# The last pair of a two-layer tower split into its two batches on separate streams, and eight heads per bank copy in the second attention

## The chip, the cores and the metric

The kernel runs on one core of one Trainium2 chip. The metric is the device time of one execution in microseconds; lower is better. It is written in Bass: each engine (PE for matmuls, ACT, DVE, POOL, and SP as a DMA queue) gets its own instruction stream in a fixed order, and the engines meet at semaphores. An instruction that waits holds all that is queued behind it on its engine.

## The reference

Eight sequences of 256 tokens by 256 features pass through two layers, each a token mixer and a feed-forward part with a layer norm after each:

```python
h = L0_tok(x)                                  # state-space mixer, 64 states per token
h = layernorm(h + L0_attn(h))                  # causal attention, 8 heads of 32, with a rank-one bias
# L0_ffn: norm, 32 heads of 8 (full attention), residual, then experts by position:
xe = xf.reshape(2, 8, 128, 256)                # tokens in order: 8 experts of 128 tokens, twice
y  = gelu(xe @ w1[e] + b1) @ w2[e] + b2
h = layernorm(h + y)
# L1_attn: gated linear attention, 4 heads of 32 keys and 64 values, a scan over 256 tokens
S = exp(gk_t) * S + k_t v_t ;  o_t = q_t S ;  o = rmsnorm(o) * gw * silu(g)
h = layernorm(h + o @ Wo)
# L1_ffn: softmax gate over 8 experts (256 -> 1024 -> 256, relu), the best two, weighted
h = layernorm(h + sum_k top_probs[k] * expert[topk_idx[k]](h))
```

All is float32.

## The kernel before

The program has three parts. `s4_tokens` computes the state-space mixer. `main_loop` computes everything up to the gate of the last feed-forward part. `expert_mixture` then runs 39 tiles of 128 gathered token rows through the expert that each tile belongs to, with all eight experts' matrices (16 MB) resident, and combines the two results per token.

`main_loop` works on four pairs of batches (pair p holds batches p and p + 4), 512 tokens each, in four blocks of 128. There are two sorts of work. The attention slots (stream x) handle two heads each: scores, their maxima on DVE (line 1715), transposed scores, exp on ACT (1543), and values (1207). X0 is the causal attention of layer 0 (8 slots per pair), X1 the 32-head attention in its feed-forward part (32 slots per pair, 16 per batch). Side stages are everything else: Y3 (projections for X0), Y2 or Y2d (from X0's output to X1's input), Y1a (X1's output projection, the positional experts' two products with GELU between, layer norm, called h2), Y1b (gated linear attention, its projection and norm, called h3, and the gate with its counts and scatters). `Plan.ORDER` puts the side stages on two streams: a has Y3, Y2 and Y1b of pair 2, b has Y1a and Y1b of pairs 0 and 1, Y1a of pair 2, then Y1a and Y1b of pair 3.

The order of the streams among each other is fixed at build time. `Plan.STAGES` lists the slots of each stage with estimated costs on PE, DVE and ACT and the names of the banks they take; `Plan.needs` lists which slot may only be ordered after which; `Plan.schedule` walks through a model of the three engines and picks at each step the slot that could begin first, among near equals the one with the longest tail. Every engine follows this one order (`weave`). The side stages share two accumulator banks (ps6, ps7), handed out in turn as tickets (`take`, 1260), so a bank's next user waits for the eviction of the user before last, on whichever stream that was.

X1's values of four heads (a quad) are gathered in bank ps4, 32 rows for each. Each quad ends in an ACT copy to `acc` (1534), two PE transposes (`outputs_t`, 1229), a DVE reciprocal of the softmax sums and a product (`normalise`, 1749). POOL prepares padded values of eight heads in `vpad` (`pad`, 1053): eight columns of values and one of ones in 32.

Y1a of pair 3 can only begin when all of X1 of pair 3 is normalised, and Y1b of pair 3 follows it. Where this leaves PE without work, `busy_last` (1281) issues filler matmuls (line 1279), 44 in all, each of 512 columns, seen in the trace as two records. The four 1 MB matrices of a pair's two positional experts pass through the two buffers of `wexp` (`load_w`, 916). The expert matrices of the last part are loaded when h2 of pair 3 and the gate of pair 2 are done (`y1b` of SP, 1016), since their room overlaps buffers of the main loop. After the gate of a pair, POOL scatters its rows into slots by expert, 8 indirect DMAs per pair (1068); the main loop ends when all have landed.

## Time and profile before

| | us |
|---|---|
| median of 3 runs | 1294.23 |
| lowest, highest | 1287.56, 1296.31 |
| the profiled execution | 1290.59 |
| its span, first to last instruction | 1288.8 |
| PE busy in the span | 1076.3 (84%) |
| DVE, ACT, POOL busy | 714.7, 481.5, 239.4 |

The rows further down are from the profiled execution. Times in them count from the start of the span. PE is the matmul part of TensorE, PEld its weight loads, which overlap the matmuls. Busy PE time includes the pipeline's depth, and filler matmuls. PEclk is the granted clock as a share of 2.4 GHz. The main loop lies between about 117 and 966 us, the expert tiles between 967 and 1252.

### The profile page before, as it was taken

The numbers are of one execution on the slowest core, as the hardware profiler recorded it, in microseconds if no ns is written. First come the engines' busy times: TensorE is split into PE (matmuls) and PEld (weight loads), VectorE is DVE, ScalarE is ACT, GpSimd is POOL, SyncE is SP. The second block draws the span as 40 slices with busy tenths as digits, with TensorE's granted clock in tenths as the row PEclk, the third lists the DMA queues.
The fourth block names the chain that finished last, engine by engine and source line by source line (L and its number), as shares of the span: only waits on it lengthen the run. The fifth ranks groups of instructions, "written<-read, shape, count | busy, mean of one in ns | idle before, by whom it ended". The sixth has DMA issues, their size and how long they took to land. (4 is left out here: it accounts for less than half of the span.)

```text
span 1288.8 us, 23098 instructions
## 1 busy us (share of the span) xinstructions
PE 1076.3 (84%) x8482; PEld 771.6 (60%) x8482; DVE 714.7 (55%) x1793; ACT 481.5 (37%) x970; POOL 239.4 (19%) x269
## 2 busy tenths in 40 slices
PE   1227997987999888889988988888889999999990
PEld 1124665544666456666455654674548999999980
DVE  7992444565555766747677556355443444444445
ACT  2111332444465443346533565343003333333332
POOL 3960000000000001201011100012123333333320
PEclk7557998988999989889987999798889999999995
DMA  5023141018521479122805220022941111111105
GB/s 170 18 52 127 65 183 33 17 37 161 67 75 63 184 218 112 35 67 74 164 1 83 64 93 1 1 66 84 379 159 34 34 42 34 41 36 38 38 30 200
DMA packets 73421, 108.90 MB, mean 84 GB/s; under 512 B 16592, under 2 KB 58336, under 8 KB 72864
## 3 DMA queue, kind: packets, MB, share of 16 engines
q1 hardware_dynamic: 66192, 74.75, 23.2%
q0 software_dynamic: 5280, 14.57, 3.5%
q10 hardware_dynamic: 1840, 18.10, 3.4%
q8 instruction: 71, 1.16, 0.4%
q14 instruction: 38, 0.31, 0.1%
HBM read 83.47 MB, written 40.97 MB: 97 GB/s over the span
## 5 line engine op out<-in xcount | busy, mean ns | idle before, releaser
L1715 DVE TENSOR_REDUCE mx<-scores_ps 128x4 f32<-128x1024 f32 (+1 forms) x160 | 186.8, 1168 | 89.3 <-PE scores_ps L1190 45.0
L1543 ACT ACTIVATE pt<-turned_ps 128x1024 f32<-128x1024 f32 (+1 forms) x160 | 157.9, 987 | 152.7 <-PE turned_ps L1186 92.2
L2255 PEld LDWEIGHTS x_ps<-x_xtT,x_w1s 128*128 128x128 f32 x1248 | 145.3, 192 | 3.4 <-ACT x_xtT L2283 1.5
L2255 PE MATMUL x_ps<-x_xtT,x_w1s 128*128 128x128 f32 x1248 | 145.9, 275 | 1.0 <-ACT x_xtT L2283 1.0
L2269 PE MATMUL x_ps<-x_experts,x_hT 128*128 x624 | 141.0, 379 | 0.0
L2269 PEld LDWEIGHTS x_ps<-x_experts,x_hT 128*128 128x128 f32 x624 | 115.6, 190 | 14.1
L1176 PE MATMUL turned_ps<-q,k 32*128 32x256 f32 x512 | 69.2, 346 | 31.1 <-DVE mx L1715 14.9
L1176 PEld LDWEIGHTS turned_ps<-q,k 32*128 32x128 f32 x512 | 42.1, 196 | 85.1 <-issue 47.2
L2298 ACT ACTIVATE x_hT<-x_ps,x_b1c 128x128 f32<-128x128 f32 x312 | 84.9, 382 | 16.9 <-issue 13.8
L2318 DVE COPY x_w1s<-x_experts 128x2048 f32 x39 | 55.5, 1424 | 49.5 <-PE x_ps L2255 37.4
L2343 DVE TENSOR_TENSOR x_y<-x_ps,x_b2b 128x256 f32<-128x256 f32 x39 | 16.5, 424 | 113.2 <-PE x_ps L2269 113.2
L1225 PE MATMUL ps<-pt,vpad 128*32 128x256 f32 x1024 | 78.5, 430 | 0.6 <-issue 0.6
L2283 ACT COPY x_xtT<-x_ps 128x256 f32<-128x256 f32 x39 | 14.5, 372 | 166.3 <-PE x_ps L2234 166.3
L1060 POOL COPY vpad<-v 128x64 f32<-128x64 f32 x64 | 13.1, 235 | 328.7 <-PE ps L1225 313.7
L2222 POOL DMA_INDIRECT y_rows<-x_y,x_row x39 | 39.2, 1006 | 180.3 <-DVEq L2348 180.3
L1164 PE MATMUL scores_ps<-k,q 32*128 32x256 f32 x512 | 69.3, 348 | 2.0 <-DVE mx L1715 1.2
L481 PE MATMUL s_ps<-s_pw,s_cs 64*32 64x64 f32 x512 | 14.7, 298 | 63.1 <-DVEq L383 58.7
L1397 PE MATMUL ps<-wexp,hid 128*128 128x256 f32 x256 | 61.7, 395 | 3.2 <-issue 3.2
L2212 POOL DMA_INDIRECT x_xt<-x_slots,x_source x39 | 59.8, 1532 | 16.9 <-issue 11.6
L1385 PE MATMUL ps<-tt_b,wexp 128*128 128x256 f32 x256 | 61.2, 389 | 0.4 <-DVE tt_b L1785 0.4
L1397 PEld LDWEIGHTS ps<-wexp,hid 128*128 128x128 f32 x256 | 49.6, 198 | 13.9 <-issue 6.8
L1186 PE MATMUL turned_ps<-mrow,pick 32*128 32x512 f32 x256 | 55.6, 419 | 0.0
(423 smaller groups left out, 1971.2 us busy)
## 6 DMA issues: line engine op xcount, KB each, us to landing
x_slots<-x_slots ACTq DMA_DIRECT2D x4, 4160.0 KB
wexp<-in_L_ffn_w SPq DMA_DIRECT2D x16, 1024.0 KB, 5.6
x_experts<-in_L_ffn_W SPq DMA_DIRECT2D x16, 1024.0 KB, 13.7
q<-heads SPq DMA_DIRECT2D x48, 128.0 KB, 5.3
k<-heads SPq DMA_DIRECT2D x48, 128.0 KB, 9.8
ha<-h SPq DMA_DIRECT2D x16, 256.0 KB, 3.2
x_pair<-y_rows SPq DMA_DIRECT2D x4, 1024.0 KB, 8.9
heads<-nat_k_hi SPq DMA_DIRECT2D x12, 256.0 KB, 4.1
```

Of the source, the lines that this page charges most:

```text
L1164: last = mm(bank[:, qb * T:(qb + 1) * T], q1[r, u.bb, u.tile, qb * P:(qb + 1) * P], k1[r, u.bb, u.tile, :], start=True, stop=True)
L1176: mm(bank[:, kt * T:(kt + 1) * T], k1[r, v.bb, v.tile, kt * P:(kt + 1) * P], q1[r, v.bb, v.tile, :], start=kt == 0, stop=False, skip_group ...
L1186: mm(bank[:, :].rearrange("p (k n) -> p k n", k=2), which, rows.unsqueeze(1).to_broadcast([32, 2, T]), start=False, stop=True, skip_group_ ...
L1225: last = mm(rows[:, 0:T], vpad[:, (pads[w.group] - 1) % 2, kt, w.n, :], data[:, kt * T:(kt + 1) * T], start=kt == 0, stop=kt == 1)
L1385: last = mm(bank[:, (f % 2) * T:(f % 2 + 1) * T], w1[:, c, f * P:(f + 1) * P], mv_[c], start=c == 0, stop=c == DC - 1)
L1397: last = mm(bank[:, 0:D], hid[:, e, f, bb * P:(bb + 1) * P], w2[:, f, :], start=f == 0, stop=f == FT0 - 1)
L1543: sc.activation(pt[v.index // 2 % (PT_RING // 2)][:, :, 0:wide], turned_ps[:, :, 0:wide], ACT.Exp)\
L1715: v.tensor_reduce(mx[:, u.group % 2, 0:blocks, u.n:u.n + 2].rearrange("p b n -> p n b"), scores_ps[:, :, 0:blocks * (P if u.causal else T) ...
L2212: g.indirect_dma_start(out=xt[:, i % XR, :], out_offset=None, in_=xs[:, :], in_offset=bass.IndirectOffsetOnAxis(mx.source[:, i:i + 1], 0))\
L2255: last = mm(ps[2 * (i % 2) + f // KH][:, f % KH * P:(f % KH + 1) * P], w1s[:, i % 2, c, f * P:(f + 1) * P], xtT[:, i % 2, c, :], start=c = ...
L2269: last = mm(ps[4 + (i - 1) % 2][:, 0:D], hT[:, (i - 1) % 2, f, :], w2[:, bass.ds(last_expert, 1), f, :], start=f == 0, stop=f == FT - 1)
L2298: sc.activation(hT[:, i % 2, f, :], ps[2 * (i % 2) + f // KH][:, f % KH * P:(f % KH + 1) * P], ACT.Relu, bias=b1c[:, bass.ds(expert * FT + ...
```

## The change

It has two parts.

In X1, two quads (eight heads) share one bank. POOL writes the values of heads 4 to 7 of a group into columns 16 to 23 of their 32, with the ones in column 24, and zeros stand elsewhere; PE adds the second quad's products onto the first's (`begins`), and only the end of the group leads to a copy, transposes, one reciprocal over 16 sums, and two products.

Pair 3 is divided into its two batches, parts 3 and 4, with stages Z1a and Z1b that work on two blocks of 128 tokens in place of four. Batch 0 stays on stream b; batch 1 goes to a new stream c. They use halves of the same buffers (`hid_half`, `lin_half`, halves of tt_b, yb_b, ob), with semaphores of their own per stream. The second expert's matrices of pair 3 go into `qk0` and `v0`, whose users are done by then, so both batches find all four resident. The expert matrices of the last part are loaded when both h2 and the gate of pair 2 are done. 36 fillers remain, on part 4 alone.

```diff
-             "b": (("Y1a", 0), ("Y1b", 0), ("Y1a", 1), ("Y1b", 1), ("Y1a", 2), ("Y1a", 3), ("Y1b", 3))}
+             "b": (("Y1a", 0), ("Y1b", 0), ("Y1a", 1), ("Y1b", 1), ("Y1a", 2), ("Z1a", 3), ("Z1b", 3)),
+             "c": (("Z1a", 4), ("Z1b", 4))}
...
-        after("Y1b", 2, 18, "Y1b", 3, 3)
-        after("Y1b", 2, 22, "Y1b", 3, 21)
-        after("Y1b", 2, 26, "Y1b", 3, 23)
+        for bb in range(2):
+            after("X1", PAIRS - 1, 16 * bb + 15 + AV_LAG + 2, "Z1a", PAIRS - 1 + bb, 0)
+            after("Y1b", 2, 18, "Z1b", PAIRS - 1 + bb, 3)
+        after("Y1b", 2, 26, "Z1b", 3, 19)
+        after("Y1a", 2, 21, "Z1a", 4, 0)
+        after("Z1b", 3, 22, "Z1b", 4, 19)
...
     def w_slot(p, i):
+        if p == PAIRS - 1 and i >= 2:
+            return (qk0_[:, :, :, :].rearrange("p a c n -> p (a c n)") if i == 2 else
+                    v0_[:, :, :, :].rearrange("p b h n -> p (b h n)")), sg(f"w_last{i % 2}"), 16
...
-            if 4 * p + i >= 2:
+            if p == PAIRS - 1 and i >= 2:
+                sp.wait_ge(sg("av_done"), plan.base["X0", PAIRS - 1] + 16)
+            elif 4 * p + i >= 2:
...
+                if (stage, q) == ("Z1b", PAIRS):
+                    sp.wait_ge(sg("h2_b"), PAIRS)
+                    sp.wait_ge(sg("h2_c"), 1)
+                    sp.wait_ge(sg("slots"), PAIRS - 1)
+                    mixture.load_experts(sp)
...
             for kt in range(2):
-                last = g.tensor_copy(vpad[:, n % 2, kt, :, 0:8],
-                                     v1[:, unit.third, kt, unit.head * 8:unit.head * 8 + 64]
-                                     .rearrange("p (h d) -> p h d", d=8))
+                for e in range(2):
+                    at = (unit.head + 4 * e) * 8
+                    last = g.tensor_copy(vpad[:, n % 2, kt, 4 * e:4 * e + 4, 16 * e:16 * e + 8],
+                                         v1[:, unit.third, kt, at:at + 32].rearrange("p (h d) -> p h d", d=8))
...
-            if k:
+            begins = u.causal or not u.ends_group
+            if k and begins:
                 pe.wait_ge(sg("acc"), k)
...
                         last = mm(rows[:, 0:T], vpad[:, (pads[w.group] - 1) % 2, kt, w.n, :],
-                                  data[:, kt * T:(kt + 1) * T], start=kt == 0, stop=kt == 1)
+                                  data[:, kt * T:(kt + 1) * T], start=begins and kt == 0,
+                                  stop=u.ends_group and kt == 1, skip_group_check=True)
...
                 u = plan.last(s, AV_LAG + 2)
-                if u and u.ends_quad:
+                if u and u.ends_out:
                     outputs_t(u)
...
-        def busy_last(p, n):
-            if p == PAIRS - 1:
-                busy(ps[0], n)
+        def busy_last(part, n):
+            if part.last:
+                busy(ps[5], n)
...
-            busy_last(p, 8)
-            pe.wait_ge(sg("g_o"), p + 1)
-            yield from project(p, "p2", ob, wt.gwo, side)
+            busy_last(part, 5)
+            pe.wait_ge(sg("g_o_" + side), turn)
+            yield from project(q, "p2", ob, wt.gwo, side, blocks)
```

In Z1a each bank takes four hidden slices of 128 tokens in place of two of 256, so a batch's expert half still fills two banks of 512 columns where the pair filled four.

## Rows read from the trace of the kernel before

**Rows 1.** By stretch: busy us of PE, PEld, DVE, ACT, POOL; PEclk; DMA

```profile
207.00:767.00 560.00, 496.58 (x3955) 316.11 (x3953) 346.18 (x802) 265.89 (x412) 44.67 (x89) 0.93 0.38 87
767.00:796.00 29.00, 27.48 (x202) 12.35 (x202) 18.70 (x35) 18.46 (x33) 0.83 (x4) 1.00 0.01 1
796.00:817.50 21.50, 15.87 (x120) 8.22 (x116) 5.84 (x19) 6.79 (x10) 0.00 (x0) 0.60 0.00 0
817.50:866.00 48.50, 45.50 (x224) 38.82 (x224) 24.28 (x51) 21.22 (x31) 3.92 (x2) 0.97 0.14 44
866.00:880.50 14.50, 11.34 (x34) 7.17 (x35) 4.50 (x19) 0.58 (x1) 1.01 (x1) 0.65 0.01 1
880.50:948.30 67.80, 57.44 (x211) 32.79 (x210) 34.31 (x108) 13.44 (x29) 13.86 (x12) 0.87 0.79 280
966.70:1250.00 283.30, 282.24 (x1932) 263.68 (x1933) 128.26 (x340) 99.62 (x352) 97.09 (x76) 0.99 0.12 37
```

**Rows 2.** PE's groups, 817.5 to 966.7: busy us, mean ns, idle before

```profile
L1279 PE MATMUL scores_ps<-ident 128*128 128x512 f32 x88 | 45.8, 675 | 0.8 <-DVE g L1963 0.8
...
L1385 PE MATMUL ps<-tt_b,wexp 128*128 128x256 f32 x64 | 14.4, 381 | 0.0
...
L1302 PE MATMUL ps<-wo,tt_b 128*128 128x256 f32 x16 | 3.9, 384 | 0.9 <-DVE sd L1972 0.9
```

**Rows 3.** Timeline of PE in the tail: start us, length us, line, names, count

```profile
766.97 1.09 PE L1289 MATMUL ps<-ident,hb 128*128 128x128 f32 x8 [2.14 <-DVEq L1822]
...
817.69 1.97 PE L1289 MATMUL ps<-ident,heads_X 128*128 128x128 f32 x8 [0.56 <-DVE heads_X L1757]
...
873.65 7.02 PE L1279 MATMUL scores_ps<-ident 128*128 128x512 f32 x10
...
947.96 0.30 PE L1496 MATMUL ps<-g_both,mask_g 128*128 128x32 f32 x2
...
948.32 15.70 PE L1279 MATMUL scores_ps<-ident 128*128 128x512 f32 x36
...
966.75 0.24 PE L2238 MATMUL x_ps<-ident,x_b1r 64*128 64x64 f32 x1 [2.73 <-PEq L2086]
```

**Rows 4.** Timeline of PE around one pair of output transposes

```profile
744.94 0.44 PE L1236 MATMUL ps<-ident,acc 128*128 128x128 f32 x2
745.31 1.07 PE L1225 MATMUL ps<-pt,vpad 128*32 128x256 f32 x16
```

**Rows 5.** Waits of the weight loads, 207 to 767: us in total, times, longest

```profile
PEld turned_ps L1176 <- DVE mx L1715: 34.6, 32, 2.3
...
PEld ps L1236 <- issue: 17.2, 58, 0.8
```

**Rows 6.** Line 1715 from 740 us on: the last maxima of the last pair

```profile
L1715 DVE TENSOR_REDUCE mx<-scores_ps x14: 1207/1225/1226, 742.4 to 795.7; 128x4 f32<-128x1024 f32 x14
```

**Rows 7.** Chain that ended last: 32 records of 128 columns in the expert stage

```profile
984.26 3.57 PE x_ps L2255 x32
```

**Rows 8.** Timeline of POOL: the two roots of the last linear part

```profile
919.03 2.93 POOL L1097 TENSOR_TENSOR rs_b<-rs_b,mhalf 128x16 f32<-128x16 f32 x1 [15.36 <-DVE rs_b L1984]
...
934.22 1.01 POOL L1097 TENSOR_TENSOR rs_b<-rs_b,mhalf 128x4 f32<-128x4 f32 x1 [12.26 <-DVE rs_b L1806]
```

**Rows 9.** Line 1618, GELU: ns least/median/most, first and last start

```profile
L1618 ACT ACTIVATE hid<-hid,b1c x64: 491/493/511, 360.0 to 857.6; 128x256 f32<-128x256 f32 x64
```

**Rows 10.** DVE's groups by form: a copy and a sum from banks

```profile
L1902 DVE COPY hid<-ps 128x512 f32<-128x512 f32 x32 | 22.1, 691 | 32.1 <-PE ps L1385 30.8 <-POOL rs_a L1097 1.2
...
L1907 DVE TENSOR_TENSOR yb_b<-ps,hb 128x256 f32<-128x256 f32 x16 | 6.8, 423 | 38.0 <-PE ps L1397 37.8 <-DVE ob L1989 0.2
```

**Rows 11.** Line 1071, the last scatters: ns least/median/most, first and last start

```profile
L1071 POOL DMA_INDIRECT x_slots<-hb,g_slot x8: 956/960/1057, 952.2 to 961.2; - x8
```

**Rows 12.** SP's queue: first and last issue of expert matrices

```profile
893.46 0.43 SPq L2132 DMA_DIRECT2D x_experts<-in_L_ffn_W  x1
...
934.41 0.47 SPq L2134 DMA_DIRECT2D x_experts<-in_L_ffn_W  x1
```

More of the change, by code:

```diff
@@ L864, in main_loop, with linear, forward_side, forward_turn @@
     mhalf = sb("mhalf", [P, 16])
-    def linear(p):
-        if plan.side("Y1b", p) == "a":
+    parts = Part.all()
+    def linear(pt_):
+        if pt_.half:
+            return (plan.side("Z1b", pt_.q), *lin_half[pt_.bb])
+        if plan.side("Y1b", pt_.q) == "a":
             return "a", g4_a, qs_a, ks_a, vg_a
         return "b", g4_b, qs_b, ks_b, vg_b
+    def forward_side(pt_):
+        return plan.side("Z1a" if pt_.half else "Y1a", pt_.q)
+    def forward_turn(pt_):
+        return 1 if pt_.last else pt_.q + 1
+    def linear_turn(pt_):
+        side = linear(pt_)[0]
+        return [o.q for o in parts if linear(o)[0] == side].index(pt_.q)
     scores_ps = ctx.enter_context(nc.psum_tensor("scores_ps", [P, 2, 512], fp32))
@@ L1391, in y1a @@
                 pe.wait_ge(sem, count)
-                for bb in range(2):
-                    bank = take(f"down{e}{bb}", p)
+                for i, bb in enumerate(part.bbs):
+                    bank = take(f"down{e}" + ("" if part.half else str(bb)), q)
                     for f in range(FT0):
-                        if bb == 0 and f % 2 == 0:
-                            pe.wait_ge(sg("hidden"), (E_IT * p + e) * FT0 + f + 2)
-                        last = mm(bank[:, 0:D], hid[:, e, f, bb * P:(bb + 1) * P], w2[:, f, :], start=f == 0,
+                        if i == 0 and f % 2 == 0:
+                            pe.wait_ge(sg("hidden_" + side), (E_IT * (forward_turn(part) - 1) + e) * FT0 + f + 2)
+                        last = mm(bank[:, 0:D], h_[:, e, f, i * P:(i + 1) * P], w2[:, f, :], start=f == 0,
                                   stop=f == FT0 - 1)
@@ L1437, in y1b @@
             for h2 in range(NHG // 2):
-                busy_last(p, h2)
-                banks = [take(f"at{2 * h2}", p), take(f"at{2 * h2 + 1}", p)]
-                for tb in range(NTB):
+                busy_last(part, h2)
+                banks = [take(f"at{2 * h2}", q), take(f"at{2 * h2 + 1}", q)]
+                for tb in range(part.n):
                     for i in range(2):
@@ L1669, in y1b @@
+            sc.copy(kT[:, part.bb:part.bb + len(part.bbs), :], full("kt", q)[:, 0:len(part.bbs) * P]
+                    .rearrange("p (b k) -> p b k", k=P)).then_inc(sg("y_act_" + side), 1)
             yield from pause(4)
[L1670 to L1672 removed]
+            for i, bb in enumerate(part.bbs):
+                bank = full(f"o{i}", q)
+                square = tt[side][:, :, cols] if part.half else tt[side][:, bb, :].rearrange("p (b d) -> p b d", b=2)
+                sc.activation(square, bank[:, :].rearrange("p (b d) -> p b d", b=2), ACT.Square).then_inc(sg("y_act_" + side), 1)
@@ L1911, in y1a, with y1b @@
                     yield
-            moments("b", lead("Y1a", p, 20))
+            moments(side, lead(stage, q, len(plan.STAGES[stage]) - 2), blocks, part.at)
             yield
-            normalised("b", h, rs["b"][1])
-            signal("h2")
+            normalised(side, h, rs[side][1][:, part.at:], blocks)
+            signal("h2_" + side)
             yield
-        def y1b(p):
-            side, g4, qs, ks, vg = linear(p)
+        def y1b(part):
+            q, p, cols, blocks = part.q, part.p, part.cols, part.blocks
+            stage = "Z1b" if part.half else "Y1b"
+            roots_at = [k for (z, k) in sorted(plan.ROOTS) if z == stage]
+            side, g4, qs, ks, vg = linear(part)
+            turn = linear_turn(part) + 1
@@ L1989, in y1b @@
-            s.step(v.tensor_tensor(ob[:, :, :], ob[:, :, :], yb[side][:, :, :], ALU.mult))
-            signal("g_o")
+            for n in range(part.n // 2):
+                add_projection("p2", q, n, h, True, side, part.first)
+                yield
+            moments(side, lead(stage, q, roots_at[1]), blocks, part.at)
             yield
-            turned("p2", p, side)
+            normalised(side, h, rs[side][1][:, part.at:], blocks)
+            signal("h3_" + side)
             yield
-            for n in range(2):
-                add_projection("p2", p, n, h, True, side)
-                yield
@@ L1997, in y1b, with gate @@
-            moments(side, lead("Y1b", p, 21))
-            yield
-            normalised(side, h, rs[side][1])
-            signal("h3")
-            yield
-            yield from gate(p, side)
-        def gate(p, side):
-            E = gt.E
-            shape = [P, NTB, E]
-            lo, pr, eq, pre = (z[:, :, :] for z in (gt.lo, gt.pr, gt.eq, gt.pre))
-            m1, m2, ix, dd = (z[:, :] for z in (gt.m1, gt.m2, gt.ix, gt.dd))
+            yield from gate(part, side, stage)
+        def gate(part, side, stage):
+            E, q, p, n = gt.E, part.q, part.p, part.n
+            shape = [P, n, E]
+            lo, pr, eq, pre, oh1, oh2, both = (z[:, 0:n, :] for z in (gt.lo, gt.pr, gt.eq, gt.pre, gt.oh1, gt.oh2, gt.both))
+            m1, m2, ix, dd = (z[:, 0:n] for z in (gt.m1, gt.m2, gt.ix, gt.dd))
```

658 lines of the change are left out of this document (372 added, 286 removed).

## The prediction

> **What bounds the kernel now.** I read the busy table by stage first, then the order of PE's instructions in the late stages, then DVE, ACT and POOL at the places where PE waits.
>
> The table [rows 1] splits the run into four regimes. From 207 to 767 us PE is busy 496.6 of 560 us (89%): attention slots and side stages share it, and PE is near its limit. From 966.7 to 1250 us the expert tiles keep PE busy 282.2 of 283.3 us; the change doesn't touch them. Between lie 200 us in which the pair 3 is finished. From 767 to 796 PE is full (27.5 of 29). From 796 to 817.5 the attention drains: 15.9 of 21.5 us at a clock of 0.60, about 9.5 us of work at full clock. After that Y1a of pair 3 runs beside the end of Y1b of pair 2, with PE full until 866. Then Y1b of pair 3 runs nearly alone: in the 67.8 us from 880.5 PE shows 57.4 busy, but much of that is filler, the matmuls of line 1279. In the whole tail the filler holds PE for 45.8 us [rows 2]. Of this 7.0 us stand at 873.65 and 15.7 at 948.32 [rows 3], so 45.8 - 7.0 - 15.7 = 23.1 us fall into the last chain and its real PE work is 57.4 - 23.1 = 34.3 us, half of the time. So from 866 on the length is set by a chain of dependent steps, not by an engine. The chain starts when the last attention output is normalised (PE takes it up at 817.69) and ends with the count matmuls at 947.96 [rows 3]: 130.5 us. Counted in full-clock work, what remains of PE's real work after 817.5 is about 45.5 x 0.97 = 44.1, plus (11.3 - 7.0) x 0.65 = 2.8, plus 34.3 x about 0.9 = 31: 78 us.
>
> **The second attention's copies.** Each of the 64 quads of X1 ends in one ACT copy, two PE transposes, one DVE reciprocal and one DVE product. After the change this happens once per two quads, with two products: 32 copies, 64 transposes and 32 reciprocals go. The value matmuls stay, in number and shape. On PE one pair of transposes takes 745.31 - 744.94 = 0.37 us between its neighbours [rows 4]; with the wait of its weight loads, 17.2 us in 58 cases or 0.30 us each [rows 5], 0.67. Eight of the 64 quads fall after 767, so 28 removals lie before it: 10.4 us, at most 18.8. But a shorter slot is only worth something where PE holds it; PE also waits for the DVE maxima, 34.6 us in 32 cases [rows 5], and there the gap eats the saving. The bounds are 0 and 18.8; I take **7 us** (two thirds of 10.4). The DVE and ACT savings lie beside PE. POOL's padding copies double in number, but each group of eight heads has its own buffer one group ahead, and POOL is busy 44.7 of 560 us [rows 1]: nothing.
>
> **The first batch is moved under the attention.** Y1a of pair 3 becomes Z1a 3 (batch 0) and Z1a 4 (batch 1). Z1a 3 may start when attention slot 23 of 32 is issued. The last 14 slots have their maxima from 742.4 to 795.7 [rows 6], so slot 23 falls near 763 and Y1a 2 is through by 767: Z1a 3 starts about there. PE work of the whole Y1a 3: 14.4 us up, the same for as many columns down, 3.9 projection [rows 2], and 16 transposes at half of the 0.37 above, 3.0: 36 us; half is 18. The halves lose nothing on PE: 32 records of 128 columns take 3.57 us in the expert stage [rows 7], against 14.4 / 2 = 7.2 us for 32 of 256 columns [rows 2]. The stretch 767 to 817.5 holds 27.5 + 9.5 = 37 us of full-clock work; with 18 more, and four transpose pairs less (1.5), it is 53.5, against 50.5 us now. If PE is full, the attention ends 3 us later; bounds are -3 (the drain sped up by the full clock) and +18 (all of it in front). I take **+3**. The end of attention comes at 817.5 - 7 + 3 = 813.5.
>
> **The second batch's forward part, Z1a 4.** Its PE work is 18 us. Around it stand three evictions of some 1.1 us (a copy of 0.4 to 0.7 [rows 10] and the hand-overs, an estimate), two waits for copy and GELU of 2 us (such a copy and two or three activations [rows 9]), and moments, POOL root (1.01 us for 4 columns [rows 8]) and normalisation, 4 us: 29 us alone. Y1b 2's rest and Z1b 3 run beside it and PE will be full as it is now, so I take **36 us** (bounds 29 and 48.5, which the whole Y1a takes). GELU is cut from 256 to 128 columns, twice the instructions: a 256-column one takes 0.49 us [rows 9]; between 0.25 (no fixed part) and 0.49 (all fixed) I take 0.40, 32 x 0.40 = 12.8 us against 16 x 0.49 = 7.9 us, 5 us more on ACT, which is 21.2 of 48.5 us busy and hides it. Here a rule speaks against the change: the Trainium skill, VectorE: DVE Perf Modes, section The TRN2 errata, says that VectorE and ScalarE pay a fixed extra time per instruction on SBUF sources and wants tiles of 512 elements or more. Its ScalarE row, 224 cycles plus the elements at 1.2 GHz, would make the 128-column GELU an estimated 0.29 us, so ACT would grow by 1.5 us, not 5; no row here shows that shape. On DVE the fixed part is seen: 512 columns take 0.691 us, 256 take 0.423 [rows 10]. Two halves cost 0.16 us more than a whole, but each chain pays only one.
>
> The four matrices of the last pair lie ready, since the second two go into qk0 and v0. Today the last ones are issued as their buffer comes free, and PE doesn't wait for them: it is busy 45.5 of the 48.5 us in which they are used [rows 1]. So residency is worth nothing in itself; it allows two passes.
>
> **The second batch's linear part, Z1b 4.** Now this chain takes 67.8 us. Halving its widths saves half of PE's 34.3 us: 17; of DVE's 34.3 busy us about 13 are gate operations of pair 2 and 3 that keep their size, the other 21.5 fall to 0.6 (0.423 / 0.691): 8.7; ACT, partly beside: 2; the two POOL roots, 2.93 us for 16 columns and 1.01 for 4 [rows 8], are 0.16 us per column, so 1.28 + 0.32 = 1.6. Together 29: **39 us**. Z1b 3 runs beside it. It brings a second gate of about 37 small DVE operations (some 8.5 us, as now), four scatters and what PE work is left, 31 / 2 = 15.5 us less what fits beside Z1a 4. Bank order, DVE and POOL are in-order, so each foreign step in front of the chain delays it. Bounds: 5 us and 39 us (run one behind the other); I take **14**. The seven microseconds of filler at 873.65 disappear within this, since that wait is then filled with work; 44 fillers become 36.
>
> Count matmuls: 813.5 + 36 + 39 + 14 = 902.5 instead of 948.3, **-45.8**.
>
> **From the counts to the experts.** Now eight scatters are issued from 952.2 to 961.2, 1.28 us apart [rows 11], and the first expert instruction of PE comes at 966.75, 4.6 us after the last. Four fewer save 5.1 us. But 18 fillers stay and end at 948.32 + 15.70 = 964.0: they become the bound, 15.7 us after the counts plus 0.3. I take **-2.4**. The 16 MB of expert matrices start with Y1b 2's gate and Z1a 4's end; they are issued 893.46 to 934.41 now, 5.85 us per expert [rows 12], while a tile takes 283.3 / 39 = 7.26 us. Even with a start at 892 the first experts are there at 918; no cost.
>
> **Sum.** -45.8 - 2.4 = -48.2 us on the profiled execution of 1290.6: 1242.4. The median of the runs shown is 1294.2, 3.6 higher: 1246.0. I say **1245**.
>
> **Rivals.**
> *Close packing.* X1 saves 12 us, nothing is lost at its end, Z1a 4 takes 34 and the foreign work adds 7: 817.5 - 12 + 34 + 46 = 885.5, -62.8 - 2.4 = -65: 1229. For it: PE's real work from 755 on is 37 - 1.5 + 78 = 113.5 us, which ends at 868 without gaps. Against: three streams in fixed order through two banks. 0.17.
> *One behind the other.* The X1 saving is eaten by DVE waits, and Z1b 4's steps stand in order behind Z1b 3's: 820.5 + 36 + 39 + 39 = 934.5, -13.8 - 2.4 = -16: 1278. For it: output rows (ob), gate tiles and the running counts are shared, so vg waits for Y1b 2 and the gate of batch 1 for that of batch 0; in the present trace Y1b 2 takes 125 us under interleaving, from 767 [rows 3] to 892, when its end releases the expert loads [rows 12]. Against: its early steps need none of these. 0.20. That the overlap comes to nothing at all (within 1%) is its far end: 0.04 more.
> *Slower, by the clock.* Eight fillers go. Where PE waited on a chain the granted clock was 0.60 and 0.65 [rows 1], where it was full 1.00: these are mixtures of 1.2 and 2.4 GHz. If the tail ran wholly at 1.2 GHz, its 113.5 us would be 227, from 760 to 987: +36, 1331. It turns slower than before only if the mean over that stretch falls under 113.5 / 190.7 = 0.60; now, with half the work density, it is 0.87. The Trainium skill, TensorE: Matmul & The Clock Gate, section What's actually happening, says that half rate is the default and that activity releases the full rate; by that rule denser work should raise the clock, as it did in 817.5 to 866 (0.97). 0.03.
>
> **How the numbers follow.** Forecast 0.56, its own range 1232 to 1262; the rivals 0.17, 0.24 and 0.03. 1228 to 1270 leaves out the lower half of close packing's tail and most of the serial case: 0.8 inside. A measurement of this kernel tells about 1% (13 us) from no change. Faster: 0.56 + 0.17 + four fifths of 0.20 = 0.89; same 0.07; slower 0.04.
>
> **What would show it.** Right: reduction of the maxima of the last pair ends about 10 us before 795.7, up matmuls of 128 columns run before it does; count matmuls of batch 1 near 902; PE busy over 85% until the second batch's g_o; expert start 16 us after the counts. Wrong: X1 stages as long as before (DVE waits grown); more than 50 us between the second h2 and the counts with PE idle behind Z1b 3's gate or a POOL root; or a clock under 0.8 in the tail. The expert stage must stay at 7.26 us per tile.

## The result and the profile after

The changed kernel is slower: median 1308.7 us (1303.2 to 1313.8) against 1290.9 us (1284.0 to 1296.3) of the kernel before on the same chip, ratio 1.014 with a 95% interval of 1.010 to 1.019. The forecast was 1245 us, range 1228 to 1270. The profiled execution spans 1304.8 us, before 1288.8.

First the busy table of the kernel after, the columns as in [rows 1], cut at its own milestones: h2 of pair 2 is taken up by PE at 754.2, the last maxima come at 790.7, the last attention output is taken up at 808.8, h2 of batch 1 at 869.4, the last counts at 961.0.

```profile
207.00:754.20 547.20, 489.05 (x3909) 312.07 (x3909) 342.66 (x776) 259.20 (x385) 53.59 (x149) 0.93 0.39 91
754.20:790.70 36.50, 33.85 (x224) 18.43 (x224) 19.09 (x35) 20.30 (x39) 1.56 (x8) 0.91 0.10 36
790.70:808.80 18.10, 14.29 (x117) 7.15 (x115) 4.72 (x17) 8.28 (x11) 0.00 (x0) 0.91 0.00 1
808.80:869.40 60.60, 49.29 (x266) 37.75 (x267) 26.76 (x58) 23.08 (x49) 4.30 (x3) 0.86 0.00 1
869.40:961.00 91.60, 65.00 (x235) 42.13 (x233) 44.68 (x176) 12.89 (x35) 18.75 (x19) 0.74 0.37 134
985.30:1265.00 279.70, 279.16 (x1920) 263.56 (x1921) 126.08 (x338) 98.31 (x348) 91.16 (x72) 0.99 0.12 36
```

Against [rows 1]: the attention stage got 12.8 us shorter, more than I had taken (7), and the attention ends at 808.8 instead of 817.7. The expert stage is as it was but for some 3 us in its first tiles. The rest is lost between: from the end of attention to the last counts it took 130.3 us before, 152.2 now, and I had forecast 89. PE is busy 65.0 of the last 91.6 us at a granted clock of 0.74, where the single chain of before had 57.4 of 67.8 at 0.87.

The timeline of PE in the tail, the columns of [rows 3]:

```profile
754.20 1.09 PE L1362 MATMUL ps<-ident,hb 128*128 128x128 f32 x8 [2.46 <-DVEq L1926]
...
808.79 0.63 PE L1362 MATMUL ps<-ident,heads_X 128*128 128x128 f32 x4 [0.61 <-DVE yb_b L2017]
...
851.83 0.44 PE L1362 MATMUL ps<-ident,hb 128*128 128x128 f32 x2 [1.98 <-DVEq L1926]
...
860.25 1.97 PE L1362 MATMUL ps<-ident,ob 128*128 128x128 f32 x8
...
869.42 0.60 PE L1362 MATMUL ps<-ident,hb 128*128 128x128 f32 x4
...
921.02 0.64 PE L1577 MATMUL ps<-g_both,mask_g 128*128 128x32 f32 x2 [4.78 <-DVE g_both L2163]
...
947.74 0.61 PE L1577 MATMUL ps<-g_both,mask_g 128*128 128x16 f32 x2 [4.77 <-DVE g_both L2163]
...
961.04 0.40 PE L1577 MATMUL ps<-g_both,mask_g 128*128 128x16 f32 x2 [0.56 <-DVE g_both L2163]
961.28 0.37 PE L1578 MATMUL ps<-g_both,onesr 128*128 128x16 f32 x2
961.51 15.70 PE L1352 MATMUL ps<-ident 128*128 128x512 f32 x36
977.67 0.24 PE L2364 MATMUL x_ps<-ident,x_b1r 64*128 64x64 f32 x1 [0.47 <-PEq L2212]
...
984.14 0.69 PE L2360 MATMUL x_ps<-ident,x_xt 128*128 128x128 f32 x2 [3.45 <-DMA x_xt<-x_slots,x_source]
```

The rows are, in order: h2 of pair 2, the last attention output, h2 of batch 0, the output projection of Y1b 2, h2 of batch 1, and the three gates: pair 2 (32 columns), batch 0, batch 1. The gate of pair 2 comes 33 us later than its 888.2 of before; the three gates follow one another, and PE stands 4.8 us at the head of its queue for each of the first two.

**Where it is lost.** I cut the tail of each trace into stretches of about 4 us and multiplied PE's busy time less filler with the granted clock of the stretch. That gives its work in us at full clock; the rest of its busy time is what the low clock cost. "Copies alone" is the unsplit kernel of the first experiment below, whose attention stage is like that of the kernel after. From h2 of pair 2 to the last counts, us:

| | length | work | low clock | filler | PE idle |
|---|---|---|---|---|---|
| before | 181.0 | 113.2 | 14.1 | 30.0 | 23.7 |
| copies alone | 179.6 | 112.4 | 14.9 | 30.6 | 21.8 |
| after | 206.8 | 117.1 | 23.5 | 21.9 | 44.4 |

The work is about what I had reckoned (113.5). Against the copies alone the tail is 27.2 us longer: 22.6 more of waiting, 8.6 more by the low clock, 4.7 more work, 8.7 less filler. And little of the work moved: under the attention (754 to 809) PE does 43.9 us of it instead of 35.5, but behind the end of attention 74.0 remain of 76.6. Of batch 0's forward part only the first expert got under the attention. Each batch has 64 records of up matmuls; behind 808.8 stand 96, batch 1's own and 32 of batch 0's. PE's groups from 808.8 to 961 (count, busy us, mean ns, idle before):

```profile
L1465 PE MATMUL ps<-tt_b,qk 128*128 128x128 f32 x64 | 9.3, 305 | 0.6 <-DVE yb_b L2017 0.6
...
L1465 PE MATMUL ps<-tt_b,wexp 128*128 128x128 f32 x32 | 3.7, 275 | 0.0
```

**How the chains hold each other.** One place read closely. DVE, ACT and PE each follow one order in which the steps of three chains take turns. On PE's timeline batch 1's output matmuls end at 916.25:

```profile
914.71 1.54 PE L1548 MATMUL ps<-vg_half,g_half 128*128 128x64 f32 x8
```

ACT's timeline at that place, the squares of batch 1 and then the exponential of pair 2's gate:

```profile
916.29 0.60 ACT L1765 ACTIVATE tt_b<-ps 128x512 f32<-128x512 f32 x1 [10.71 <-PE ps L1548]
...
917.25 0.24 ACT L1775 ACTIVATE g_pr<-g_lo 128x32 f32<-128x32 f32 x1
```

DVE's timeline. The product at 913.02 is batch 1's (that of batch 0 came at 896.30); it stands behind DVE's wait for batch 0's root. Then come pair 2's gate, batch 0's two products and the first sum of batch 1:

```profile
910.93 0.19 DVE L2141 TENSOR_TENSOR g_lo<-g_lo,g_m 128x32 f32<-128x32 f32 x1
...
913.02 0.69 DVE L2092 TENSOR_TENSOR ob<-ob,gwb 128x512 f32<-128x512 f32 x1 [1.75 <-POOL rs_b L1170]
917.59 0.18 DVE L2147 TENSOR_REDUCE g_m<-g_pr 128x4 f32<-128x32 f32 x1 [3.88 <-ACT g_pr L1775]
...
920.96 0.68 DVE L2106 TENSOR_TENSOR yb_b<-yb_b,rs_b 128x512 f32<-128x512 f32 x1
...
922.55 0.69 DVE L2099 TENSOR_REDUCE rs_b<-tt_b 128x8 f32<-128x512 f32 x1 [0.17 <-DVE ob L2109]
```

Batch 0's product at 920.96 needs a root that POOL delivered at 913.0. It stands behind pair 2's gate. That gate's exponential needs a result that DVE gave at 911.1, but on ACT it stands behind the squares of batch 1, which wait 10.7 us for batch 1's output matmuls on PE, until 916.3. So batch 0 waits 8 us for pair 2, which waits for batch 1. And batch 1, the last chain, pays too: its squares are there at 916.9, the sum over them comes at 922.55, 5.7 us later, behind pair 2's gate and batch 0's products. No step here is long; each chain pays for the latency of the others. What is shown is the order of the engines' queues. How much the two accumulator banks add, which the three streams share, no run tells apart.

### The profile page after: what moved, and what is told of

It is laid out like the page before. It is cut to its first block and busy times, and to the rows that moved or that the text cites. A ratio compares the mean times of both kernels' runs of the same rounds, so it can differ in the third digit from the quotient of the medians.

```text
span 1304.8 us, 23159 instructions
## 1 busy us (share of the span) xinstructions
PE 1075.9 (82%) x8484; PEld 775.6 (59%) x8484; DVE 717.9 (55%) x1819; ACT 478.1 (37%) x971; POOL 248.8 (19%) x340
## 5 line engine op out<-in xcount | busy, mean ns | idle before, releaser
L2381 PEld LDWEIGHTS x_ps<-x_xtT,x_w1s 128*128 128x128 f32 x1248 | 148.0, 195 | 3.6 <-ACT x_xtT L2409 1.6
L2395 PEld LDWEIGHTS x_ps<-x_experts,x_hT 128*128 128x128 f32 x624 | 115.6, 190 | 14.1
L1134 POOL COPY vpad<-v 128x32 f32<-128x32 f32 x128 | 22.8, 222 | 313.7 <-PE ps L1297 298.9
L1170 POOL TENSOR_TENSOR rs_b<-rs_b,mhalf 128x4 f32<-128x4 f32 (+3 forms) x13 | 17.0, 1309 | 199.8 <-DVE rs_b L1908 145.7
L1465 PE MATMUL ps<-tt_b,wexp 128*128 128x256 f32 (+1 forms) x256 | 53.5, 359 | 0.1
L482 PEld LDWEIGHTS s_ps<-s_pw,s_cs 64*32 64x32 f32 x512 | 11.7, 135 | 64.9 <-issue 37.5
## 6 DMA issues: line engine op xcount, KB each, us to landing
x_experts<-in_L_ffn_W SPq DMA_DIRECT2D x16, 1024.0 KB, 14.1
```

Source lines behind the costliest of these rows:

```text
L1465: last = mm(bank[:, i * wide:(i + 1) * wide], w1[:, c, f * P:(f + 1) * P], mv_[c], start=c == 0, stop=c == DC - 1)
L2381: last = mm(ps[2 * (i % 2) + f // KH][:, f % KH * P:(f % KH + 1) * P], w1s[:, i % 2, c, f * P:(f + 1) * P], xtT[:, i % 2, c, :], start=c = ...
L2395: last = mm(ps[4 + (i - 1) % 2][:, 0:D], hT[:, (i - 1) % 2, f, :], w2[:, bass.ds(last_expert, 1), f, :], start=f == 0, stop=f == FT - 1)
```

## The experiments

Milestones in us of each profiled execution; "attention end" is where PE takes up the last attention output, "h2" where it takes up h2 of the last chain, "Y1b 2" are the counts of pair 2, "first up" is the first up matmul of the expert tiles. Ratios are medians to the kernel before on the same chip, with their 95% interval; executions of one kernel spread over 4 to 18 us, and a profiled one can lie as far as 11 us off its median.

| kernel | h2 pair 2 | attention end | h2 | Y1b 2 | last counts | first up | ratio |
|---|---|---|---|---|---|---|---|
| before | 767.0 | 817.7 | 880.5 | 888.2 | 948.0 | 972.2 | 1 |
| after | 754.2 | 808.8 | 869.4 | 921.0 | 961.0 | 985.3 | 1.014 [1.010, 1.019] |
| e1_heads | 754.3 | 804.4 | 867.4 | 875.1 | 933.9 | 958.2 | 0.982 [0.978, 0.987] |
| e2_split | 764.9 | 817.0 | 877.9 | 929.5 | 969.7 | 993.6 | 1.016 [1.011, 1.021] |
| e3_nofill | 753.4 | 808.1 | 866.6 | 918.2 | 956.3 | 982.6 | 1.008 [1.005, 1.012] |
| e4_linear_first | 755.4 | 834.6 | 883.1 | 888.5 | 965.1 | 987.2 | 1.018 [1.011, 1.025] |
| e5_serial | 761.6 | 841.1 | 931.4 | 902.8 | 977.4 | 999.4 | 1.015 [1.011, 1.019] |
| e6_heads_trim | 752.7 | 803.1 | 859.8 | 870.1 | 928.1 | 952.3 | 0.985 [0.982, 0.988] |
| e7_resident | 755.3 | 805.8 | 868.4 | 876.1 | 932.9 | 957.0 | 0.987 [0.984, 0.990] |
| e8_late_load | 756.3 | 805.8 | 869.5 | 877.2 | 937.2 | 965.1 | 0.992 [0.990, 0.995] |
| e9_forward | 755.5 | 809.8 | 859.5 | 918.8 | 950.1 | 981.0 | 1.006 [1.003, 1.009] |
| e10_no_batch0 | 756.6 | 812.2 | 868.4 | 885.4 | 919.0 | 943.8 | (less work) |
| e11_more_fill | 756.2 | 810.8 | 871.3 | 917.2 | 956.5 | 981.6 | 1.021 [1.014, 1.027] |
| e12_forward_y1b2 | 760.4 | 818.1 | 888.5 | 904.4 | 953.6 | 977.9 | 1.007 [1.004, 1.011] |

**The copies alone, and the split alone.** e1 takes the hunks of the second attention into the kernel before (`vpad` with its nine ones, `ends_out`, `begins`, the 16 sums in `rc`); e2 takes all the others.

> The kernel before with the eight heads per bank copy alone; the last pair stays whole. My step 'X1 copies' said 7 us of gain, with bounds 0 and 18.8. In the profile of the changed kernel h2 of pair 2 comes at 754.2 us where it came at 766.97, so theory A (the copies are worth all of that, the loss lies in the split alone): 12 to 13 us faster than before, near 1278. Rival R (part of the 12.8 us comes from other tail priorities of the order, or is given back where the last chain begins): 0 to 6 us faster.

> The changed kernel with a copy per four heads as before, so the split alone. Theory A (the two parts add up): the split alone costs the 16 to 18 us seen plus the 12.8 us of the copies, so about 29 us slower than before, near 1320. Rival R (the freed slots of the second attention are taken by the first batch's work, so that the copies and the split work together): 18 us slower or less.

The copies are worth 20 us (1274.5 against 1294.2; in e7, on another chip, 17), the split costs 20 (1314.5). Neither is what its theories had (12 to 13 or at most 6 us for the copies, 29 or at most 18 for the split), but the loss is the split's. In e1 the 12.7 us that the copies gain ahead of h2 of pair 2 arrive whole at the experts (14 us earlier); in the kernel after, against e2, 8.3 of 10.7 do. Together the two give +1.4% where their sum would be about 0; I have no run that tells why the copies are worth less beside the split.

**The fillers.** e3 keeps only the 18 behind the counts; e11 lets batch 0's waits have them too.

```diff
-            if part.last:
+            if part.last and n == 18:                             # e3
+            if part.last or part.q == PAIRS - 1 and n < 18:       # e11
                 busy(ps[5], n)
```

> The changed kernel without the 18 filler matmuls that stand in front of the last part's waits; the 18 after its counts stay. The output is the same. Theory F (with three streams the fillers stand in front of other streams' work, which now waits 0.87 to 1.5 us for each; 6.0 us of them stand from 948.6 to 954.5 ahead of the last gate's transposes): 5 to 12 us faster than the changed kernel. Rival C (the clock, 0.56 to 0.87 in the stretches after 869 us, falls further without them): 3 to 15 us slower, with the count matmuls later and the clock in 869 to 961 lower.

> The kernel after with the filler matmuls doubled: those that stand ahead of the waits of batch 1's linear part now also stand ahead of the same waits of batch 0's (18 more, of 0.44 us at full clock each). The granted clock over 869 to 961 was 0.74 in the kernel after. Theory C (the low clock in the tail is what costs): the clock over the linear parts rises to 0.85 or more and the last counts come 5 us or more earlier than 961; ratio to before 1.010 or less. Theory H (PE in order, waits of the chains, not its speed): the clock rises but the last counts come within 3 us of 961 or later, up to 8 us later, since each filler stands ahead of foreign steps; ratio 1.014 to 1.021.

The linear parts of e3 in the busy table (columns of [rows 1]):

```profile
866.60:956.30 89.70, 51.23 (x206) 37.48 (x204) 46.73 (x182) 13.94 (x38) 18.77 (x19) 0.64 0.36 128
```

The same stretch of e11:

```profile
871.30:956.50 85.20, 66.19 (x266) 39.41 (x264) 45.29 (x176) 12.91 (x35) 18.73 (x19) 0.92 0.39 140
```

The clock went from 0.74 to 0.64 and to 0.92, and the chain from 91.6 us to 89.7 and 85.2. So e3 lost clock and no time: its median is 5 us under that of the kernel after, the least that theory F had, with intervals that overlap. The profiled e11 gains 6 us in the chain, but its median of 1313.5 shows no gain (theory C needed a ratio of 1.010 or less; 1.021 is in the range of theory H). How much of the 6 us is real stays open; of the 38 us that this chain took beyond the forecast, a clock of 0.92 gives back 6 at the most.

**The order.** Three kernels keep all the work and change only what waits for what.

```diff
+        after("Y1b", 2, 18, "Z1a", 4, 0)                           # e4
-        after("Z1b", 3, 22, "Z1b", 4, 19)
+        after("Z1b", 3, 22, "Z1b", 4, 0)                           # e5
```

> The changed kernel with one more condition of order: batch 1's forward part (Z1a 4) is ordered only after slot 18 of Y1b 2 (its p2 transposes), so that the linear part of pair 2 is finished earlier. Theory O (three gates in series hang on Y1b 2, whose count matmuls came at 921.0 us where they came at 888.2 before; the order starves it): Y1b 2's counts 15 to 30 us earlier, the last counts 8 to 15 us earlier than 961.0. Rival C (what lengthens the tail is PE at half clock and its idle time as such, not who is first): within 3 us of the changed kernel. Rival W (batch 1's chain was the longest): slower by the 5 to 10 us by which it starts later.

> The kernel after with one more constraint on the order: the linear part of batch 1 (Z1b 4) begins only after the last step of batch 0's (Z1b 3). Nothing is left out. It measures the term of my sum that was 39 us: Z1b 4 alone, from its h2_t transposes to its counts. Theory I (the halves are short, 39 to 45 us alone, and what went wrong is only that three streams wait for each other in a fixed order): Z1b 4 takes 39 to 45 us here; batch 0's counts, without foreign steps, come near 930 instead of 947.7, and the last counts near 972; the kernel is about 11 us slower than after (ratio to before near 1.023). Theory L (a chain of steps keeps most of its length when its tiles are halved): Z1b 4 takes 55 to 62 us alone, of 67.8 for the whole pair in the kernel before; the last counts come near 990 and the ratio is near 1.037.

In e4 pair 2's gate is back at 888.5, yet the last counts come 4 us later, as rival W had it: the attention is pushed back (its last output transposes come at 827.9, 806.0 in the kernel after), and its output is taken up 26 us later. In e5 batch 1's linear part runs alone, from 931.4 to 977.4: 46.0 us. This is the term that I had put at 39 and theory L at 55 to 62. And e5, with the two half chains strictly one behind the other, has the ratio of the kernel after (1.0149, 1.0144): running them side by side gained nothing that can be measured. It isn't a clean test of the linear parts alone, though. The order of the earlier stages changed with the one constraint: the attention's end moved from 808.8 to 841.1, and batch 0's counts came at 925.3, 22 us earlier than in the kernel after.

**Batch 0's linear part left out.** e10 drops Z1b 3 from the order; its 256 tokens have no gate, no scatters and no part in the experts, and its output rows are copies of another batch's.

> The kernel after with the linear part, the gate and the scatters of batch 0 of the last pair left out (its forward part stays; its rows of the output are another batch's, and its tokens are missing among the experts). It asks whose steps stand in front of the last chain, which takes 91.6 us from its h2 transposes (869.4) to its counts (961.0) in the kernel after and 46 when held back until batch 0 is through. Theory Z (batch 0's chain): the last chain takes 42 to 50 us and its counts come at 905 to 918. Theory Y (the rest of Y1b 2, whose counts came at 921): the last chain still takes 60 us or more and its counts come at 930 or later. My forecast of the kernel after had this chain at 39 us with 14 more for batch 0.

Its last chain, timeline of PE:

```profile
868.42 0.60 PE L1363 MATMUL ps<-ident,hb 128*128 128x128 f32 x4
...
903.87 0.66 PE L1363 MATMUL ps<-ident,ob 128*128 128x128 f32 x4 [1.11 <-DVEq L1927]
...
919.01 0.29 PE L1578 MATMUL ps<-g_both,mask_g 128*128 128x16 f32 x2
```

50.6 us instead of 91.6, and pair 2's gate back at 885.4. Theory Z holds, with the end 1 us outside its bounds: batch 0's half chain costs the last one 41 us, where I had 14. That is batch 0's own steps together with the delay that they put on pair 2: Y1b 2's projection comes at 846.9 instead of 860.3 without them, and its counts 36 us earlier; e10 doesn't separate the two. But Z1a 4 still takes 56.2 us (812.2 to 868.4) beside Y1b 2 and the rest of Z1a 3.

**Only the forward part split.** e9 has Z1a 3 and Z1a 4, but one linear chain for the whole pair; its comparison is e6, the unsplit kernel with the same fillers.

```diff
-             "b": (("Y1a", 0), ("Y1b", 0), ("Y1a", 1), ("Y1b", 1), ("Y1a", 2), ("Z1a", 3), ("Z1b", 3)),
-             "c": (("Z1a", 4), ("Z1b", 4))}
+             "b": (("Y1a", 0), ("Y1b", 0), ("Y1a", 1), ("Y1b", 1), ("Y1a", 2), ("Z1a", 3), ("Y1b", 3)),
+             "c": (("Z1a", 4),)}
...
-            after("Y1b", 2, 18, "Z1b", PAIRS - 1 + bb, 3)
-        after("Y1b", 2, 26, "Z1b", 3, 19)
+        after("Y1b", 2, 18, "Y1b", 3, 3)
...
+        after("Z1a", 4, len(self.STAGES["Z1a"]) - 1, "Y1b", 3, 0)
+        after("Y1b", 2, 17, "Z1a", 3, 7)                           # e12 only
```

> Only the forward part of the last pair is split (Z1a 3 under the attention, Z1a 4 after it, all four matrices resident, eight-head copies); its linear part stays whole, one chain for both batches as in the kernel before, with the fillers of the trimmed version (none ahead of h2, 8, 4 and 2 ahead of the later waits). Nothing is left out. Theory I (what costs is that the linear part became two chains that wait for each other; the forward split gains what I forecast for it): end of attention near 809, Z1a 4 some 42 us, h2 of both batches ready near 851 to 858, then about 62 us for the whole chain as in the trimmed unsplit version (859.8 to 928.1 there is 68.3), last counts 915 to 922, 6 to 13 us earlier than that version's 928.1, ratio to before near 0.975. Theory P (the third stream itself costs: it pushes Y1b 2 back, and the vg steps of the last chain wait for it): Y1b 2's output projection comes at 855 to 860 instead of 833, the last counts fall at 926 or later, and the ratio is 0.983 or more.

> The kernel of e9 (forward part split, linear part whole) with one more constraint on the order: the second expert of batch 0's forward part (Z1a 3) waits until the normalised output of Y1b 2 is there, so that Y1b 2 is no longer pushed back by batch 0. In e9 Y1b 2's output projection came at 872.5 and its counts at 918.8, against 832 and 870.1 in the trimmed unsplit version, and the last chain took 90.6 us instead of 68.3. Theory Q (Y1b 2's delay is what lengthens the last chain, and it can be had back without giving the early forward part away): Y1b 2's projection comes at 835 to 848, the last chain takes 66 to 75 us, the last counts come at 922 to 935, ratio to before 0.98 to 0.99. Theory S (the three streams share a fixed amount of time: whatever is put first, another is pushed back by as much): Y1b 2 comes early, but Z1a 4 ends at 875 or later, and the last counts stay at 942 or later, ratio 1.000 or more, as happened when Y1b 2 was put ahead of Z1a 4 in the fully split kernel.

This was the surprise. e9 is 26 us slower than e6 (1298.6 against 1272.1, on different chips; both times the kernel before had 1292): the forward split alone costs more than the split linear part adds to it (10 us, to 1308.7). h2 comes at the same time as in e6 (859.5, 859.8), so the work done under the attention bought nothing, but Y1b 2 is pushed back by 49 us, and the last chain, whose vg steps wait for it, takes 90.6 us instead of 68.3. Theory P, larger than I put it. Its expert loads are late too (issued from 924.6), and from the counts to the experts it takes 30.9 us, 6.7 more than in e6. Two waits of PE in e9:

```profile
872.54 1.97 PE L1364 MATMUL ps<-ident,ob 128*128 128x128 f32 x8 [4.46 <-DVEq L1932]
...
918.75 0.63 PE L1583 MATMUL ps<-g_both,mask_g 128*128 128x32 f32 x2 [4.78 <-DVE g_both L2169]
```

e12 was to give Y1b 2 its turn back, and hardly did: its projection comes at 867.0, 5.5 us earlier than in e9, where e6 has it at 832.0, and its counts at 904.4 against 870.1. The last chain is short again (65.1 us), but Z1a 4 ends 29 us later and the counts come at 953.6. Theory Q is out; of theory S the late end of Z1a 4, the late counts and the ratio are as it had them, the early Y1b 2 isn't. In e4 and e9 what is put first is gained and what is put second is lost, and e12 gained little and lost more. Three orders don't prove that no order pays.

**The two things that I put at nothing.** e7 gives the unsplit kernel the two resident matrices; e8 holds the expert loads back (`filled(sp, "o0", p)` ahead of `load_experts`).

> The kernel before with the eight-head copies, unsplit, and with the one other part of the change that can stand alone: the second expert's two matrices of the last pair go to the memory of qk0 and v0 and are loaded there during Y1a of pair 2, beside the end of the attention. I put that at nothing. Theory N (nothing): Y1a 3 keeps its place and length (transposes at about 804, h2_t at 867), ratio 0.982 as with the copies alone, within 0.004. Theory M (the earlier loads, some 2 MB beside the attention, collide with other transfers, or PE did wait for the late ones): the end of attention moves by more than 2 us or Y1a 3 is shorter by more than 2 us, and the ratio differs from 0.982 by more than 0.004.

> The kernel before with the eight-head copies, unsplit, and with the loads of the sixteen experts' matrices held back until batch 0's output matmuls of the last pair are issued, some 20 us later than they could start, so that they still run when the first expert tile begins, as in the kernel after. Nothing is left out. Theory N (a late load costs nothing while it stays ahead of the tiles, as I put it): from the last counts to the first expert up-matmul 24.2 us as now, and the span as with the copies alone, 1275. Theory D (the load stands in front of the first gathers): the first gather takes about 5.8 us instead of some 3, the first up-matmul comes 26 to 28 us after the counts, and the span grows by 2 to 4 us (ratio 0.984 to 0.986).

e7 equals the copies alone within the intervals: residency is worth nothing, as forecast. e8 is 6 us slower than e7 on the same chip (1281.7 against 1275.6), outside what theory D had. In the traces its counts come 4.3 us later than in e7 and the experts 3.8 us later behind them. Of the 4.3 us, 2.3 are the last gate step, from the transposes of h3 to the counts: 8.5 us in e7, but 10.8 in e8, e1 and the kernel before. The rest I can't account for. POOL's timeline between the last scatter and the first gather, in e1:

```profile
947.17 0.96 POOL L1074 DMA_INDIRECT x_slots<-hb,g_slot  x1 [0.30 <-issue]
953.40 1.74 POOL L2223 DMA_INDIRECT x_xt<-x_slots,x_source  x1 [5.27 <-POOLq L2097]
```

In e8, and PE's first instruction of the expert stage there:

```profile
950.41 0.96 POOL L1075 DMA_INDIRECT x_slots<-hb,g_slot  x1 [0.30 <-issue]
959.91 1.74 POOL L2224 DMA_INDIRECT x_xt<-x_slots,x_source  x1 [8.54 <-POOLq L2098]
...
959.25 0.34 PE L2250 MATMUL x_ps<-ident,x_b1r 64*128 64x64 f32 x1 [6.00 <-PEq L2098]
```

In the kernel after:

```profile
968.71 0.96 POOL L1144 DMA_INDIRECT x_slots<-hb,g_slot  x1 [0.30 <-issue]
978.33 1.73 POOL L2338 DMA_INDIRECT x_xt<-x_slots,x_source  x1 [8.66 <-POOLq L2212]
```

In e4, the split kernel whose last load is issued at 934.43, with the same instruction of PE:

```profile
972.83 0.96 POOL L1145 DMA_INDIRECT x_slots<-hb,g_slot  x1 [0.30 <-issue]
982.26 1.73 POOL L2339 DMA_INDIRECT x_xt<-x_slots,x_source  x1 [8.47 <-POOLq L2213]
...
981.61 0.24 PE L2365 MATMUL x_ps<-ident,x_b1r 64*128 64x64 f32 x1 [0.30 <-PEq L2213]
```

At the end of the main loop all engines meet. In e8 PE is through with its fillers 6.0 us before that point opens, so the scatters hold it up, and they land 3.3 us later than in e1 while the expert matrices stream. In the kernel after the wait of POOL looks the same and isn't: PE's fillers end at 977.21 and the expert stage begins at 977.67, and in e4 and e5, where no expert matrix is under way any more, POOL waits 8.5 and 8.4 us all the same. There the four scatters are early and the 18 fillers behind the counts set the end, as I had forecast. What the late load costs in the kernel after stands behind that. It is issued from 927.95 to 970.56, since it waits for pair 2's late gate ([rows 12]: 893.46 to 934.41), and the first gather takes 5.8 us from its issue to PE's transposes, 3.9 in e1, e4 and e5. From the counts to the first up matmul it is 24.3 us, 22.1 in e4 and 22.0 in e5: 2.2 us.

**Faster than both.** e6, the kernel before with the copies and without the fillers that stood ahead of h2, runs at 1272.1 us, ratio 0.985 [0.982, 0.988].

```diff
-            busy_last(p, 5)
             pe.wait_ge(sg("h2"), p + 1)
...
-            busy_last(p, 6)
+            busy_last(p, 4)
             pe.wait_ge(sg("h3"), p + 1)
...
-            busy_last(p, 4)
+            busy_last(p, 2)
             pe.wait_ge(sg("g_both"), p + 1)
```

> The kernel before with the eight-head copies and without the split, and with fewer filler matmuls in the last pair's linear part: the 5 ahead of the wait for h2 go, the 6 ahead of h3 become 4, the 4 ahead of the gate's result become 2. In the version with all fillers h2 stood ready at about 858.6 and PE took it up at 867.4, behind 6.5 us of filler. Theory F (these fillers stand in the chain): h2_t comes about 6 us earlier and the last counts 7 to 9 us earlier than 933.9; ratio to before near 0.977 against 0.982 with all fillers. Theory K (the fillers hold the clock up, and without them the steps that follow run at a lower clock and give it back): the last counts within 3 us of 933.9, a mean clock over 867 to 934 that is lower by 0.05 or more, and a ratio of 0.982 or above.

Its h2 comes 7.6 us and its last counts 5.8 us earlier than in e1; on one chip it beats the untrimmed e7 by 3.5 us. The fillers ahead of a wait that is already over stand in the chain, as theory F had it, but part is given back: the clock over the last chain is 0.83 instead of 0.87 (e1). The ratio of 0.985 is the one of theory K, and e1 itself (0.982) lies within the interval, so the gain is shown against e7 alone; both are well ahead of the two kernels compared.

## Why the prediction was wrong, point by point

- *What bounds the tail.* Right: from the end of attention on it is a chain of dependent steps. I then computed with the chain as if it were work: I took off the halved busy time of PE, DVE and ACT in full.
- *The copies, 7 us.* Mis-sized: 12.8 us in the attention stage, 0.46 us per removed copy and transposes, inside the bounds of 0 and 18.8. I had cut the saving because PE also waits for the maxima; those waits stayed as they were (33.6 us in 32 cases, 34.6 in [rows 5]), so the gap ate nothing. PE's busy time fell by 7.5 us, the other 5.3 were waiting. e1 puts the whole part at 20 us in the median.
- *The attention's end, +3.* Right: 54.6 us from h2 of pair 2 to it, against 50.1 in e1, so +4.5. But the reason I gave, 18 us of work going in, was wrong: 8 went in.
- *Z1a 4, 36 us.* Failed: 60.6, outside the bounds. The step that failed is "PE will be full as it is now": between 808.8 and 869.4 PE works 49.3 of 60.6 us, and the second half of batch 0's forward part lies in that stretch too. The upper bound of 48.5 was misread as well: it is a stretch of [rows 1] up to 866, while the whole Y1a takes 53.5 us from the attention's end (817.7) until its normalised h2 is there (871.2), and 62.8 until PE takes it up (880.5). So half of Y1a in the new kernel takes as long as all of it did. The 7.0 us of filler at 873.65, which I took for a wait that other work would fill, stood behind h2 already: that wait was over.
- *GELU at 0.40 us for 128 columns.* Right: 32 of them take 0.387 us each (below). The estimate from the Trainium skill, VectorE: DVE Perf Modes, section The TRN2 errata, was 0.29; the measurement decides. Nor was it this that cost the time: behind the attention ACT is busy 36.0 of 152.2 us.
- *Z1b 4 alone, 39 us.* A little low: 46.0 in e5, 50.6 beside Y1b 2 in e10. A half chain is 0.68 of a whole (67.8).
- *Batch 0 beside it, 14 us, bounds 5 and 39.* The largest miss and the step that failed most: 41 us against e10 and 46 against e5, over the upper bound that I took as "one behind the other". It fell on the low side because I counted only what batch 0 adds in work, not that its steps, pair 2's and batch 1's wait for each other in every queue. The kernel with the two half chains in series (e5) is as fast as the one with them side by side.
- *Counts to experts, -2.4.* Right for what I had computed: PE's first expert instruction comes 16.6 us behind the counts, forecast 16.4, before 18.8, and the fillers are the bound. But the first up matmul comes 24.3 us behind them, as before (24.2), since the gather behind that instruction is slow. The step that failed is "even with a start at 892, no cost": the start came at 928, and a load still under way costs 2.2 us here (against e4 and e5); in e8, where it also holds up the scatters, 3.8 in the trace and 6 in the medians.
- *The expert stage*, put at no change: 2.9 us. Its first 32 up matmuls take 6.50 us at a granted clock of 0.56, the next 32 take 3.84 at 1.00, after PE stood 3.45 us for the gather; before, the first took 3.84 too.
- *The sum.* Attention end -4.7, Z1a 4 +24.6, last chain +38.6, counts to experts +2.5, first tiles +2.9: 64 us between -48 and +16.
- *The rivals.* "One behind the other" had the right mechanism in the linear parts (39 + 39 us there; 91.6 measured, 2 x 46) and the wrong floor (1278): it left Z1a 4 at 36 us, and its eaten gain of the copies didn't come. "Slower, by the clock" came out slower, but the lower clock is 8.6 of the 27.2 us, and its mean from 754 to 961 is 0.82, not under 0.60. Beside it no rival had a tail longer than the one before; 0.04 for slower was far too little. Of my signs of being wrong two came: 91.6 us between the second h2 and the counts, and a clock of 0.74 there.

GELU in the kernel after, the columns of [rows 9]:

```profile
L1705 ACT ACTIVATE hid_half<-hid_half,b1c x32: 385/387/403, 784.4 to 846.8; 128x128 f32<-128x128 f32 x32
```

A root of 8 columns on POOL's timeline, 1.64 us (I had taken 0.16 us per column, so 2.93 - 1.28 = 1.65) [rows 8]:

```profile
911.35 1.64 POOL L1170 TENSOR_TENSOR rs_b<-rs_b,mhalf 128x8 f32<-128x8 f32 x1 [18.62 <-DVE rs_b L2104]
```

## What to carry to other kernels

Where a stretch is set by latency, halving the tiles doesn't halve it: here half a chain took 0.68 of a whole, and two of them on engines that work in order took more than the whole (109 us from batch 0's h2 at 851.8 to the last counts, before 67.8). Splitting pays only if the first half truly runs under other work; count first how much of it gets there (here 8 of 18 us) and what it pushes back. To estimate interleaved chains, start from the sum of their lengths alone, not the sum of their work: here 2 x 46 us against 91.6 for the last one. Even that is no upper bound, as the 109 us show. Look also at what the last moved stage releases: a load that starts 35 us later can lie on the path. And where an engine waits at a point where all meet, look at what each of the others does until then before you name the cause.

## What I had not expected of the hardware

- Indirect scatters that end while the 16 MB of expert matrices stream (364 to 399 GB/s in e8) landed late: from the last issue's end to the next step's start 8.5 us in e8 and 8.9 in e9, instead of 5.3 in e1, e7 and e12. In these kernels PE's fillers had ended before. The first gather under the same stream took 5.8 us to PE's transposes in the kernel after instead of 3.9 in e4 and e5.
- The granted clock in the linear tail was 0.64, 0.74 and 0.92 with 0, 19 and 31 us of filler in it (e3, after, e11), and the chain's length changed by 4.5 us between e3 and e11: most of it is waiting for DVE, ACT and POOL.
- One thing was as expected: halving the columns cost PE nothing as such. 32 up records of 128 columns took 3.7 us at full clock, 0.117 each, where 64 of 256 columns took 14.4, 0.225 each [rows 2]. What grew was waiting.
